# Narrower destination ranges, and picked rows laid side by side for one sum over neighbours

## The reference

```python
# layer 0, relational: each edge has one of 86 relations, 16 bases
msg  = einsum('eb,ebo->eo', w_comp[etype], einsum('ei,bio->ebo', x[src], weight))
a    = tanh(relu(sum((x[src] @ A1.T + b1) * (x[dst] @ A2.T + b2 + rel_emb[etype])) / sqrt(32)))
h    = relu(segment_sum(a * msg, dst) + x[src[last edge of dst]] @ self_loop_weight)
x    = layernorm(x + h)
# layer 1: sum of the neighbours
x    = layernorm(x + segment_sum(x[src], dst))
# layer 2: attention, a softmax over the edges of each destination
x    = layernorm(x + segment_sum(x[src] * softmax_by_dst(leaky(s_src[src] + s_dst[dst])), dst))
# layer 3: ten steps of propagation with degree norms, restart 0.1
x    = layernorm(x + propagate(x, 10))
```

## Time and profile before

| | |
|---|---|
| median of three runs | 1105.08 us |
| profiled execution | 1103.32 us |
| its span, first to last instruction | 1101.1 us |
| mean granted clock of TensorE, of full speed | 0.909 |
| PE busy | 902.0 us |
| DVE busy | 942.5 us |
| ACT busy | 533.2 us |
| POOL busy | 579.0 us |

### The profile page before, as it was taken

How to read it: one execution, slowest core, us unless ns; L and a number is a source line. 1 busy time by engine, 2 the same in 40 slices (tenths; PEclk the granted TensorE clock), 3 DMA queues, 4 the chain that set the end, 5 groups by cost and what they waited for, 6 DMA issues and landing times.

```text
span 1101.1 us, 57074 instructions
## 1 busy us (share of the span) xinstructions
PE 902.0 (82%) x24130; PEld 846.5 (77%) x24130; DVE 942.5 (86%) x2309; ACT 533.2 (48%) x1342; POOL 579.0 (53%) x546
## 2 busy tenths in 40 slices
PE   3338888988988988888888888885849958999996
PEld 3327778877877887778788778775749958999996
DVE  7959999999999999999999999996469976555556
ACT  1126565655656567767767767777675300000000
POOL 5777777777777777777777777772000000000000
PEclk9559998989989989989989989996869979999998
DMA  5253232323323333333333333320000000000001
GB/s 121 45 88 59 53 68 59 60 55 69 57 54 62 63 57 59 64 62 59 60 68 57 58 65 59 67 43 8 5 1 4 4 2 4 4 4 4 5 4 19
DMA packets 54401, 48.55 MB, mean 44 GB/s; under 512 B 35470, under 2 KB 44142, under 8 KB 54142
## 3 DMA queue, kind: packets, MB, share of 16 engines
q0 software_dynamic: 17088, 8.78, 10.6%
q10 hardware_dynamic: 11456, 22.01, 6.0%
q1 hardware_dynamic: 25598, 14.07, 5.5%
HBM read 42.49 MB, written 2.32 MB: 41 GB/s over the span
## 4 chain that ended last, share of the span: by engine, by line
DVE 51%; PE 33%; issue 7%; ACT 5%; DMA 3%; ACTq 0%; SPq 0%; DVEq 0%
PE ps L885 14%; DVE arena L1418 11%; DVE arena L1385 11%; PE ps L818 4%; PE ps L932 3%; DVE aggT L1431 3%; DVE arena L1439 3%; DVE arena L1400 2%; DVE arena L1412 2%; DVE arena L1404 2%; DVE arena L1375 2%; PE ps L916 2%; DVE arena L1362 2%; DVE arena L1448 2%; PE ps L856 2%
## 5 line engine op out<-in xcount | busy, mean ns | idle before, releaser
L632 POOL DMA_INDIRECT arena<-x_pad,arena x534 | 577.1, 1081 | 163.0 <-issue 162.4
L818 PE MATMUL ps<-aggT 128*128 128x128 f16 x3472 | 226.5, 229 | 0.0
L818 PEld LDWEIGHTS ps<-aggT 128*128 128x128 f16 x3472 | 215.8, 104 | 2.1 <-DVE aggT L1431 0.4
L1385 DVE TENSOR_SCALAR arena<-pair_no,arena 128x275 bf16<-128x275 f16 (+2 forms) x784 | 183.5, 287 | 0.0
L885 PE MATMUL ps<-arena,adj_words 128*128 128x64 f16 x5625 | 171.9, 192 | 3.4 <-DVEq L1703 3.2
L885 PEld LDWEIGHTS ps<-arena,adj_words 128*128 128x128 fp8e4 x5625 | 170.5, 97 | 4.7 <-DVEq L1703 3.6
L1418 DVE TENSOR_TENSOR arena<-ps,arena 128x1536 f32<-128x1536 f32 x98 | 171.3, 1748 | 0.2
L1080 ACT ACTIVATE adj_words<-arena 128x500 uint8 x196 | 126.6, 646 | 56.8 <-ACT arena L1055 56.0
L1050 ACT ACTIVATE arena<-ps 128x500 fp8e4<-128x500 f32 x196 | 114.3, 583 | 56.3 <-PE ps L767 34.4
L780 PE MATMUL ps<-arena 128*32 128x44 f32 (+3 forms) x7048 | 133.0, 211 | 5.4 <-DVE arena L1418 5.1
L780 PEld LDWEIGHTS ps<-arena 128*32 128x32 f32 x7048 | 109.0, 112 | 26.4 <-DVE arena L1418 8.2
(11 more groups left out here) (223 smaller groups left out, 1152.0 us busy)
## 6 DMA issues: line engine op xcount, KB each, us to landing
arena<-line_table ACTq DMA_DIRECT2D x48, 344.0 KB
arena<-x_pad,arena POOLq DMA_INDIRECT x534
arena<-pick_table SPq DMA_DIRECT2D x31, 256.0 KB
arena<-line_table ACTq DMA_DIRECT2D x48, 80.0 KB
arena<-dst_parts SPq DMA_DIRECT2D x196, 5.7 KB
agg_table<-arena SPq DMA_DIRECT2D x196, 2.5 KB
dst_parts<-aggT ACTq DMA_DIRECT2D x1, 735.0 KB, 11.4
x<-x_pad ACTq DMA_DIRECT2D x1, 400.0 KB, 13.7
```

Of the source, the lines that this page charges most:

```text
L632: pool.indirect_dma_start(to, None, table, bass.IndirectOffsetOnAxis(ap=index, axis=0)).then_inc(done, 16)
L818: mm = nc.tensor.matmul(ps[:, at:at + PICK_WIDE * FEAT], pick_hot[:, u % PICK_RING, k * P:(k + 1) * P], x_parts[:, t, j * PICK_WIDE:(j + 1 ...
L1385: last = v.tensor_scalar(pair_hot[:, d % 2, k, 0:n], pair_no[:, 0:n], pair_of[:, d * DUO + k // SLOTS, k % SLOTS:k % SLOTS + 1], None, ALU ...
```

## The change

The page becomes 19 destinations, the slots start at 0, 2, 6 and 10 and have ranges of 7, 9, 9 and 9; HOTS becomes 10, and what follows from these constants follows: 175, 225, 225 and 250 pair columns, 475 columns of counts, 105 rows of the fetch, PIECES_FROM 43 and 70.

In `x_parts` the four blocks of a quad now lie innermost, so that for each feature its four candidates are neighbours. PE's product is of the same size, with its columns in that order. The mask is applied in one multiplication of the same size as before, and the two additions become one reduction over the innermost four, `add_picked`, which stands behind the pair one-hots and raises `pick_read` there. `x_parts` is filled in eight operations, two for each place in the quad, in place of two.

```diff
--- before.py
+++ after.py
@@ -42,11 +42,11 @@
 GROUPS = -(-TILES // SLOTS)
 WINDOW = SLOTS * P
 GROUPED = GROUPS * WINDOW
-PAGE = 20
-STARTS = (0, 1, 5, 9)
-WIDTH = 11
+PAGE = 19
+STARTS = (0, 2, 6, 10)
+WIDTH = 9
 HOTS = WIDTH + 1
-PAIR_DSTS = (8, WIDTH, WIDTH, HOTS)
+PAIR_DSTS = (7, WIDTH, WIDTH, HOTS)
 PAIRS = PAGE * BLOCKS
 DUO = 2
 DUOS = GROUPS // DUO
@@ -283,7 +283,9 @@
         pick_mask = stay.cut(PICKS * WIDE * PICK_WIDE, F16).rearrange("p (c k w) -> p c k w", c=PICKS, k=WIDE)
         pick = Carver(aggT, NODES_PAD)
         pick.at = NODES_PAD - 2 * PICK_DEEP * PICK_WIDE * FEAT // 2
-        x_parts = pick.cut(2 * PICK_DEEP * PICK_WIDE * FEAT, F16).rearrange("p (t b f) -> p t b f", t=2, f=FEAT)
+        x_words = pick.cut(2 * PICK_DEEP * PICK_WIDE * FEAT, F16)
+        x_parts = x_words.rearrange("p (t j f w) -> p t j w f", t=2, f=FEAT, w=PICK_WIDE)
+        x_quad = x_words.rearrange("p (t j c) -> p t j c", t=2, c=FEAT * PICK_WIDE)
         pick.at = 0
         pick_hot = pick.cut(PICK_RING * DUO * WINDOW, F16).rearrange("p (j e) -> p j e", j=PICK_RING)
         q_parts = aggT[:, 0:BLOCKS * 3 * REL_COLS // 2 + 1].bitcast(BF16)[:, 0:BLOCKS * 3 * REL_COLS]\
@@ -816,8 +818,7 @@
                         at = PICK_AT_BANK + k * PICK_WIDE * FEAT
                         for t in range(2):
                             mm = nc.tensor.matmul(ps[:, at:at + PICK_WIDE * FEAT], pick_hot[:, u % PICK_RING, k * P:(k + 1) * P],
-                                                  x_parts[:, t, j * PICK_WIDE:(j + 1) * PICK_WIDE, :]
-                                                  .rearrange("p b f -> p (b f)"),
+                                                  x_quad[:, t, j, :],
                                                   start=(j == 0 and t == 0 and k % SLOTS == 0),
                                                   stop=(j == PICK_DEEP - 1 and t == 1 and k % SLOTS == SLOTS - 1))
                     mm.then_inc(pick_used, 1)
@@ -1319,10 +1320,12 @@
                     link(v.tensor_scalar(pick_mask[:, first::every, :, w], own, float(w), 1.0 / PICK_SCALE,
                                          ALU.is_equal, ALU.mult))
             dve.wait_ge(x_loaded, 16)
-            link(v.memset(x_parts[:, :, BLOCKS:PICK_DEEP * PICK_WIDE, :], 0.0))
-            link(v.tensor_scalar(x_parts[:, 0, 0:BLOCKS, :], x[:], PICK_SCALE, None, ALU.mult))
-            link(v.scalar_tensor_tensor(out=x_parts[:, 1, 0:BLOCKS, :], in0=x[:], scalar=PICK_SCALE,
-                                        in1=x_parts[:, 0, 0:BLOCKS, :], op0=ALU.mult, op1=ALU.subtract))
+            link(v.memset(x_parts[:, :, PICK_DEEP - 1], 0.0))
+            for w in range(PICK_WIDE):
+                of = x[:, w::PICK_WIDE, :]
+                high, low = [x_parts[:, t, 0:-(-(BLOCKS - w) // PICK_WIDE), w, :] for t in range(2)]
+                link(v.tensor_scalar(high, of, PICK_SCALE, None, ALU.mult))
+                link(v.scalar_tensor_tensor(out=low, in0=of, scalar=PICK_SCALE, in1=high, op0=ALU.mult, op1=ALU.subtract))
 
             dve.wait_ge(q_made, 1)
             split(link, q_whole, q_rest, [q_parts[:, :, j, 0:SCORED] for j in range(3)])
@@ -1431,25 +1434,19 @@
                     v.tensor_scalar(pick_hot[:, u % PICK_RING, :], codes[:, c % 2, :], pick_no[:, j:j + 1], None, ALU.is_equal)\
                      .then_inc(pick_hots, 1)
 
-                picked_of = picked.rearrange("p (k w f) -> p k w f", k=WIDE, w=PICK_WIDE)
-
                 def mask_picked(c):
                     dve.wait_ge(pick_used, PICK_DEEP * (c + 1))
-                    n = [P, WIDE * PICK_WIDE, FEAT]
-                    step(v.tensor_tensor(picked.rearrange("p (w f) -> p w f", f=FEAT),
+                    n = [P, WIDE, FEAT, PICK_WIDE]
+                    step(v.tensor_tensor(picked.rearrange("p (k f w) -> p k f w", k=WIDE, w=PICK_WIDE),
                                          ps[:, PICK_AT_BANK:PICK_AT_BANK + WIDE * PICK_WIDE * FEAT]
-                                         .rearrange("p (w f) -> p w f", f=FEAT),
-                                         pick_mask[:, c].rearrange("p k w -> p (k w)").unsqueeze(2).to_broadcast(n), ALU.mult))
-
-                def add_halves():
-                    half = PICK_WIDE // 2
+                                         .rearrange("p (k f w) -> p k f w", k=WIDE, w=PICK_WIDE),
+                                         pick_mask[:, c].unsqueeze(2).to_broadcast(n), ALU.mult))
+
+                def add_picked(c):
                     chain.wait()
                     dve.sem_inc(pick_read, 1)
-                    step(v.tensor_tensor(picked_of[:, :, 0:half], picked_of[:, :, 0:half], picked_of[:, :, half:PICK_WIDE], ALU.add))
-
-                def add_pairs(c):
-                    chain.wait()
-                    step(v.tensor_tensor(xp[:, PICKED[c] % AHEAD, :, 0:FEAT], picked_of[:, :, 0, :], picked_of[:, :, 1, :], ALU.add))
+                    step(v.tensor_reduce(xp[:, PICKED[c] % AHEAD, :, 0:FEAT],
+                                         picked.rearrange("p (k f w) -> p k f w", k=WIDE, w=PICK_WIDE), AX.X, ALU.add))
 
                 make_lines(0)
                 make_dst_hot(0)
@@ -1469,12 +1466,10 @@
                         mask_picked(picked_now)
                     if more:
                         make_rows(d + 1)
-                    if picked_now is not None:
-                        add_halves()
                     if more:
                         make_pairs(d + 1, 6, WIDE)
                     if picked_now is not None:
-                        add_pairs(picked_now)
+                        add_picked(picked_now)
                     if d % LINE_DUOS == 1 and c + 1 < LINES:
                         make_dst_hot(c + 1)
                     for n in own[0:1]:
```

## The result

The changed kernel takes 1254.95 us (median of four runs, 1252.24 to 1256.46) against 1104.69 before: a ratio of 1.136 (95% interval 1.134 to 1.138), so 150 us slower where I had forecast 28 faster. The profiled execution took 1252.24 us, its span 1250.4.

What follows compares the result with a forecast made beforehand. It took DVE to bound the sweep until another engine's slack was used up; -26.1 - 3.3 - 1.6 - 5 + 6.7 + 3.8 - 2 = -27.5 us from 1103.3 gave a forecast of 1076 us, range 1067 to 1088.

Steps and rivals of the forecast that it cites:

- the last line on the narrower ranges: Side load, line load and store: one row less in each was costed at nothing.
- rival 1: In the sweep, another engine takes part of the gain, with waits at low clock: 12 us lost, 1088 us; chance 0.24.
- Rival 2: In the picks, the reduction pays for each short row of four: +36 us, 1112 us, slower; chance 0.04.
- The reduction: Sum over neighbours, 31 picks: 1234 ns replaces two additions of 1097 ns; +0.22 us each, +6.7 us.
- Rivals 3 and 4: 3: edges outside ranges force the general branch, 15 ms, chance 0.01; 4: all terms bad plus rival 1, 1098 us, 0.06.
- Mix product: DVE's product in the sweep, 1536 elements to 1280 over 98 duos: -26.1 us, the deciding term.
- Weighing: DVE's weighing in the sweep, 192 elements to 160, 33 ns in each of 98 duos: -3.3 us.
- One-hot of destinations: DVE's destination one-hot, 384 elements to 320, 33 ns in each of 49 lines: -1.6 us.
- Pairs: Pair one-hots in 196 groups: -5 us, bounds 0 and -9; odd widths (175, 225) might pay 11 ns extra.
- The preparation: Filling x_parts before the sweep, priced by L1319's 16-bit writes 8 bytes apart: +3.8 us, lower bound +1.4.
- The end of the sweep: Last duos: no degree-counting pieces on ACT ahead of the weights DVE waits for; -2 us, bounds 0 to -5.
- the blind sum: All terms of the forecast together, made before measuring: -27.5 us.

Runs made afterwards that it cites:

- e4: The kernel before, its computing untouched, with 19 rows instead of 20 in side load, line load and store: 1261.5 us, ratio 1.142 to before.
- e1: The changed kernel, page of 19 kept, but with 20 rows in side load, line load and store: 1090.6 us, ratio 0.988 to before.
- e10: e1 with the line load's 86 rows fetched as 80 and 6: 1082.7 us, ratio 0.983 to before.
- e16: e1 with the relation rows of the line load padded from 86 to 96: 1074.0 us, ratio 0.973 to before.
- e15: The kernel before with the relation rows of the line load padded from 86 to 96: 1101.8 us, ratio 0.9975 to before.
- e9: The changed kernel, 19 rows everywhere, with only the line load's 86 rows fetched as 80 and 6: 1076.6 us, ratio 0.975 to before.
- e14: The whole change with the line load fetched as 80 and 6, the same kernel as e9 run again: 1081.3 us.
- e3: The changed kernel with 20 rows in side and line loads only, the store keeping 19: 1156.5 us, ratio 1.047 to before.
- e5: e1 with 23 rows in the store alone: 1173.0 us, ratio 1.062 to before.
- e6: e1 with 24 rows in the store alone: 1097.2 us, ratio 0.993 to before.

## Why the prediction was wrong

**The step that failed** is the last line on the narrower ranges: "A page of 19 also means one row less in each side load, line and store: nothing, no wait of DVE ends on them in the steady part." It was right that no wait of DVE ended on them before, and wrong that this bounds them. I priced the size of the transfers (a row less) and not how they are laid out; by the packet counts the number of rows sets the number of engines, and this term of "nothing" measured +157 us alone (e4). And I named no cover: SP's store waited 139.2 us for the store before it already, a row of the trace that the argument never used, and what SP's queue holds behind that wait (the pick codes) was never named. With stores of 20 rows the three duos of lead that the codes have covered that wait; with 19 rows they did not, and DVE waited 161 us. The sign that I had named, waits of DVE above 15 us in the sweep with a clock clearly below 0.94, came.

**The bound.** "One nanosecond less on DVE is one less in the time, until another engine's slack is used up" looked at engines only. SP's queue, which the busy table does not list, was the nearest thing to a second bound: in e1, with 20 rows and DVE faster, DVE waits again for codes (12.9 us as "issue" and 1.3 at the transfer, 75 to 760 us, in an execution of 1085.8 us). That is about the 15 us between e1's median and the forecast, and it is rival 1 in another place than I put it. The 5.5 us for the last load of `agg`, which the expectation of e10 counts in, cost nothing: DVE's next wait for PE, 13.3 us in the kernel before, is 7.9 us there, so that the two together are 13.4 us. So 20 rows would not have saved the forecast: e1, at 1090.6 us, is outside its range too, and the change is worth 14 us on it.

**The rivals.** None had this mechanism, and the 0.01 for what I did not see was far too little. Rival 2 (rows of four) is refuted: the reduction takes 1207 ns. Rivals 3 and 4 did not occur. The clock, in rival 1, fell (0.94 to 0.80 in the window) as an effect. Two readings of the earlier trace rows were wrong, without weight for the outcome: the clock stands at 8 tenths in 7 slices of the sweep, not in 12 to 16, so that rival 1's price of 12 us was too high by its own working, and behind the sweep DVE has two slices at 9.

**The terms, by shape.** The groups of e16 from 100 to 700 us, for the earlier trace rows:

```profile
L1426 DVE TENSOR_TENSOR arena<-ps,arena 128x1280 f32<-128x1280 f32 x88 | 130.1, 1478 | 0.0
L1439 DVE TENSOR_SCALAR aggT<-arena,pick_no 128x1024 f16<-128x1024 f16 x206 | 99.9, 496 | 1.6
L1393 DVE TENSOR_SCALAR arena<-pair_no,arena 128x225 bf16<-128x225 f16 x351 | 89.6, 288 | 0.0
L1393 DVE TENSOR_SCALAR arena<-pair_no,arena 128x250 bf16<-128x250 f16 x175 | 51.5, 294 | 0.0
L1393 DVE TENSOR_SCALAR arena<-pair_no,arena 128x175 bf16<-128x175 f16 x176 | 46.3, 263 | 0.0
L1453 DVE TENSOR_REDUCE arena<-arena 128x256 f32<-128x1024 f32 x30 | 36.2, 1207 | 0.0
L1420 DVE TENSOR_TENSOR arena<-arena 128x160 f32<-128x160 f32 x88 | 27.4, 312 | 5.9 <-ACT arena L1105 5.7
L1374 DVE TENSOR_TENSOR arena<-next_no,arena 128x320 bf16<-128x320 bf16 x44 | 13.7, 312 | 0.0
```

- Mix product: 1478 ns for a forecast of 1480; -26.4 us.
- Weighing: 361 to 312, -49 ns where I had -33: -4.8 us. One-hot of destinations: -38 ns, -1.9 us.
- Pairs: 175 columns save 8 ns, 225 save 7, but 250 cost 294 where 300 cost 288. A group saves 8 + 14 - 6 = 16 ns: -3.1 us, inside the bounds, by another pattern than the odd widths.
- The reduction: 1207 - 1097 + 80 = +0.19 us a pick, +5.9.
- The preparation, in the changed kernel's timeline:

```profile
45.33 0.27 DVE L1323 MEMSET aggT<- 128x256 f16 x1 [0.42 <-DVE arena L1320]
45.64 0.65 DVE L1327 TENSOR_SCALAR aggT<-x 128x224 f16<-128x224 f32 x1
46.32 0.66 DVE L1328 SCALAR_TENSOR_TENSOR aggT<-x,aggT 128x224 f16<-128x224 f32 x1
47.01 0.38 DVE L1327 TENSOR_SCALAR aggT<-x 128x192 f16<-128x192 f32 x1
...
49.58 0.58 DVE L1328 SCALAR_TENSOR_TENSOR aggT<-x,aggT 128x192 f16<-128x192 f32 x1
```
  From 45.33 to 50.16 is 4.83 us where it was 1.77, and the wait of 0.42 ahead of it was 0.09: +3.4 us, near the row of L1319 and not near the price without a step.
- Not foreseen: the mean of the pick one-hot went from 482 to 496 ns (x217, +3 us) with the same shape. The median is 479 ns in the kernel before and in the changed one, so a few long ones make the difference.

The end of the sweep lost its 4.30 us wait: in e16 no weighing waits more than 1.8 us for ACT. With every transfer of both kernels on enough engines the change is worth 1074.0 - 1101.8 = -27.8 us (e16 against e15), where the blind sum had -27.5. The terms as measured, with -4.3 for the end, add up to -28.2 us. So the price of each part was sound, but that the totals agree within 1 us is partly luck, since misses of 1 to 3 us in the terms cancel. And it was the sum of another kernel than the one changed: on its own line load, even with 20 rows, the change is worth 14 us (e1).

**What stays open.** Why the runs of the kernels with the cut line load spread over up to 16 us (e9 and e14, one kernel, have 1071.8 to 1087.0 in six runs). Why some one-hots of equal shape take longer. By which path one more issue on ACT costs. How much of the delay was the side loads' and how much the line load's page rows'. Which engines a transfer used.

## What to carry to other kernels

When a change alters a size, look at every transfer whose rows follow from it, and factor the number: 20 to 19 took these, by the packet counts, from ten engines to one, and cost 157 us with nothing else changed (e4). List what stands behind each wait of a queue that has no busy time of its own, as SP's here, and how much lead it has, before calling an engine the only bound. A load whose row count has few divisors (86) is a burden on its engines for every small transfer that shares them; padding it to 96 cost nothing here (e15).

## What the runs showed of the hardware that was not expected

- Rows of a transfer and time, all else equal: stores of 19, 23 and 24 rows gave 1156.5, 1173.0 and 1097.2 us (e3, e5, e6), with 20 rows 1090.6 (e1).
- The packet counts of all runs differ as if a transfer of n rows had n + k packets, with k the largest divisor of n up to 16: 19 + 1, 23 + 1, 20 + 10, 24 + 12, 32 + 16, 86 + 2, 96 + 16. So the counts on two pages show a change of k.
- Two queues took turns packet by packet: a store of 19 packets of 128 bytes went one packet every 0.16 us while a line load ran, and within 0.19 us when none did. One landed 9.63 us behind its issue; once the line load was spread, SP waited 4.2 us at the most (e9).
- Splitting one transfer in two in ACT's fixed-order queue cost 9 us over 48 loads (1104 to 1113); PE's waits for ACT went from 18.5 to 33.5 us and DVE's for PE from 2.9 to 19.3.
- A float32 reduction of 1024 elements over rows of four takes 1207 ns, no more than its elements and a start by the earlier trace rows. With 16-bit values written 8 bytes apart a multiplication of 224 elements took 0.65 us and one of 192 0.38 to 0.46, where 800 elements written side by side took 0.58.
